# Quantised feed-forward stage: second norm's moments at the GELU on ScalarE, the output norm's last pass on ScalarE, the next batch's first norm ahead of the second norm

## The reference

```
def act_quant_fake(x):
    scale = 127.0 / jnp.clip(jnp.max(jnp.abs(x), axis=-1, keepdims=True), 1e-05)
    return jnp.clip(jnp.round(x * scale), -128.0, 127.0) / scale
...
h = layernorm(x, ln1_g, ln1_b)      # 256 features: "first norm"
h = bitlinear(h, w1, b1)            # act_quant_fake(h) @ ternary w1 + b1, 256 -> 1024
h = jax.nn.gelu(h, approximate=False)
h = layernorm(h, ln2_g, ln2_b)      # 1024 features: "second norm"
h = bitlinear(h, w2, b2)            # 1024 -> 256
...
x = _layernorm(x + _L1_ffn_ref(x, ...), axis=-1)   # "output norm", no gain or offset
```

## Time and profile before

| | |
|---|---|
| median of the runs | 3598.76 us (three runs: 3587.14, 3598.76, 16188.73) |
| the profiled execution | 3601.07 us |
| its span, first to last instruction | 3599.3 us |
| instructions | 49730 |
| TensorE busy | 2938.0 us (82%) |
| VectorE busy | 2760.9 us (77%) |
| ScalarE busy | 1921.6 us (53%) |
| GpSimd busy | 2071.5 us (58%) |

### The profile page before, as it was taken

The page is one execution under the profiler, slowest core; times in us unless marked ns, Lnnn a source line. Parts: engine busy times, 40 slices in busy tenths (PEclk is TensorE's granted clock), DMA queues, the critical chain, the costliest instruction groups (busy, mean ns, idle before and its releaser), DMA issues. The chain is left out here.

```text
span 3599.3 us, 49730 instructions
## 1 busy us (share of the span) xinstructions
PE 2938.0 (82%) x18386; PEld 1618.9 (45%) x18386; DVE 2760.9 (77%) x4668; ACT 1921.6 (53%) x3233; POOL 2071.5 (58%) x1116
## 2 busy tenths in 40 slices
PE   8968989657489748899999999999999999758633
PEld 3438888534367513344444443444434444234412
DVE  4566767666411129999999999999999999967588
ACT  2343333214211127678777777778777787524244
POOL 0015445312400116989999999999999999932100
PEclk8878888769699869999999999999999999978856
DMA  1000000000323243444444454444544444420000
GB/s 51 0 1 3 4 4 4 8 21 0 120 93 128 68 117 118 156 145 173 155 146 154 148 175 155 145 158 146 176 155 148 152 153 149 149 95 1 22 0 24
DMA packets 120572, 343.63 MB, mean 95 GB/s; under 512 B 14875, under 2 KB 45554, under 8 KB 119570
## 3 DMA queue, kind: packets, MB, share of 16 engines
q1 hardware_dynamic: 114450, 331.91, 27.5%
q0 software_dynamic: 3072, 6.00, 0.8%
q10 hardware_dynamic: 2816, 2.62, 0.2%
HBM read 328.21 MB, written 14.68 MB: 95 GB/s over the span
## 5 line engine op out<-in xcount | busy, mean ns | idle before, releaser
L2034 POOL TENSOR_TENSOR mb_h<-mb_h,mb_BC 128x1024 f32<-128x1024 f32 x512 | 1218.0, 2399 | 195.8 <-DVE mb_h L2326 194.6
L2326 DVE TENSOR_TENSOR_SCAN mb_h<-mb_dA,mb_bx 128x512 f32<-128x512 f32 x1024 | 1183.1, 1192 | 47.1 <-ACT mb_dA L2189 47.1
L2422 PE MATMUL mb_y<-mb_h,ident 128*128 128x512 f32 x2048 | 943.0, 605 | 57.0 <-POOL mb_h L2034 56.7
L2189 ACT ACTIVATE mb_dA<-mb_delta,mb_A 128x511 f32<-128x511 f32 x1024 | 658.0, 713 | 175.0 <-DVE mb_h L2326 171.6
L2322 DVE TENSOR_TENSOR mb_bx<-mb_du,mb_BC 128x512 f32<-128x512 f32 x1024 | 646.7, 673 | 1.9 <-ACT mb_du L2133 1.9
L2422 PEld LDWEIGHTS mb_y<-mb_h,ident 128*128 128x128 f32 x2048 | 380.5, 192 | 581.4 <-issue 422.9
L250 PE MATMUL mb_p<-mb_xT,mb_in_w 128*128 128x512 f32 x512 | 269.6, 676 | 87.7 <-ACT mb_sz L2093 81.1
L250 PE MATMUL mb_p<-mb_upad,mb_convd 128*128 128x512 f32 x512 | 225.0, 592 | 0.8 <-ACT mb_upad L2081 0.8
L250 PEld LDWEIGHTS mb_p<-mb_xT,mb_in_w 128*128 128x128 f32 x512 | 110.1, 219 | 239.7 <-issue 136.7
L1738 DVE TENSOR_TENSOR me_h<-me_s,me_p 128x320 f32<-128x320 f32 x64 | 31.2, 488 | 220.8 <-ACT me_s L1715 220.8
L1692 POOL DMA_INDIRECT me_y<-expert_results,slot x32 | 31.1, 973 | 258.1 <-DMA expert_results<-me_oe 248.7
(11 more groups left out here) (443 smaller groups left out, 5534.7 us busy)
## 6 DMA issues: line engine op xcount, KB each, us to landing
mb_BC<-mamba_BC SPq DMA_DIRECT2D x256, 1024.0 KB, 5.3
me_W<-in_L_ffn_W SPq DMA_DIRECT2D x24, 1024.0 KB, 9.4
mb_in_w<-in_L_attn_in_proj_w SPq DMA_DIRECT2D x4, 1024.0 KB, 5.1
mb_convd<-in_mamba_taps SPq DMA_DIRECT2D x4, 1024.0 KB, 7.2
expert_rows<-me_zero SPq DMA_DIRECT2D x1, 2560.0 KB, 10.1
x<-in_x SPq DMA_DIRECT2D x4, 512.0 KB, 5.5
me_xe<-expert_rows SPq DMA_DIRECT2D x8, 256.0 KB, 10.6
expert_results<-me_oe ACTq DMA_DIRECT2D x8, 256.0 KB, 7.6
```

The source lines that it names most:

```text
L2034: tt(hk, hk, buffer(k, it)[:, 1, :, :], ALU.mult).then_inc(*pos(f"hc_{k}{part}"))
L2189: i = av(dA[k % 2][:, c, s, 1:], delta[:, it % 2, mc, 1:], ACT.Exp, scale=A[:, MC * layer(it) + mc, n:n + 1])
L2326: nc.vector.tensor_tensor_scan(h[k % NBUF][:, c, s, :], dA[k % 2][:, c, s, :], bx[s][:, :], 0.0, ALU.mult, ALU.add).then_inc(*dvs(f"sc{s}_ ...
L2422: i = mm(ybank[c][:, :], m.ident[:, :], h[k % NBUF][:, c, s, :], start=False, stop=e == HALF - 1 and s == SU - 1)
```

## The change

- The second norm's moments are taken on ScalarE. Each GELU also sums its output into `sums`; a Copy makes minus the mean of it (`mv[:, q, 0:1]`), and a Square of h2 with that as bias sums the squared deviations into `mv[:, q, 1:2]`. `second_stats` and its semaphore are gone. `second_sqrt` takes the root with scale 1/1024 and epsilon as bias. `affine` adds the (negative) mean of the second norm where it subtracted it.
- `last_norm` is split: VectorE makes the reciprocal and `shift`, minus mean times reciprocal; ScalarE makes the four passes of 128x256 as x * rstd + shift.
- On VectorE `first_quantised(b+1)` stands ahead of `second_norm(b)`.
- On ScalarE `second_sqrt(b+1)` stands directly behind `gelu(b+1)`, and `last_norm(b-1)` ahead of `scaled(b)`.

```diff
@@ -2831,7 +2831,8 @@
-        stats, mv, sd, rstd = (sb(f"qf_{n}", s) for n, s in (("stats", [P, TPB, 2, 6]), ("mv", [P, TPB, 2]), ("sd", [P, TPB]), ("rstd", [P, TPB])))
+        sums, mv, sd, rstd = (sb(f"qf_{n}", s) for n, s in (("sums", [P, TPB]), ("mv", [P, TPB, 2]), ("sd", [P, TPB]), ("rstd", [P, TPB])))
+        squares, eps, shift = sb("qf_squares", [P, HF]), sb("qf_eps", [P, 1]), sb("qf_shift", [P, TPB])
...
@@ -2867,7 +2868,7 @@
-                    sp.wait_ge(*dve3.at("out", b))
+                    sp.wait_ge(*act4.at("out", b))
@@ -2891,11 +2892,18 @@
                 def gelu(j):
                     for q in tl:
                         a.wait_ge(*dve_e.at(f"e{q}", j))
-                        av(h2[:, j % 2, q, :], h2[:, j % 2, q, :], ACT.Gelu).then_inc(*act1(f"g{q}"))
+                        if q == 0:
+                            a.wait_ge(*dve2.at(f"g{TPB - 1}", j - 1))
+                        av(h2[:, j % 2, q, :], h2[:, j % 2, q, :], ACT.Gelu, accum_out=sums[:, q:q + 1]).then_inc(*act1(f"g{q}"))
+                        a.wait_ge(*act1.at(f"g{q}", j))
+                        av(mv[:, q, 0:1], sums[:, q:q + 1], ACT.Copy, scale=-1.0 / HF).then_inc(*act1(f"m{q}"))
+                        a.wait_ge(*act1.at(f"m{q}", j))
+                        av(squares[:, :], h2[:, j % 2, q, :], ACT.Square, bias=mv[:, q, 0:1], accum_out=mv[:, q, 1:2]).then_inc(*act1(f"v{q}"))
 
                 def second_sqrt(b):
-                    a.wait_ge(*dve_st.at("eps", b))
-                    av(sd[:, :], sd[:, :], ACT.Sqrt).then_inc(*act2("sqrt"))
+                    a.wait_ge(*act1.at(f"v{TPB - 1}", b))
+                    a.wait_ge(*dve2.at("rstd", b - 1))
+                    av(sd[:, :], mv[:, :, 1], ACT.Sqrt, scale=1.0 / HF, bias=eps[:, 0:1]).then_inc(*act2("sqrt"))
 
                 def scaled(b):
                     a.wait_ge(*dve2.at("rec", b))
@@ -2918,8 +2926,15 @@
                     a.wait_ge(*dve3.at("eps", b))
                     av(lnc.sd[:, :], lnc.sd[:, :], ACT.Sqrt).then_inc(*act4("sqrt"))
 
+                def last_norm(b):
+                    a.wait_ge(*dve3.at("shift", b))
+                    for q in tl:
+                        i = av(tile(b, q), tile(b, q), ACT.Identity, scale=lnc.rstd[:, q:q + 1], bias=shift[:, q:q + 1])
+                    i.then_inc(*act4("out"))
+
                 first_sqrt(0)
                 first_half(0)
+                a.wait_ge(ident_made, 1)
                 gelu(0)
                 second_sqrt(0)
                 for b in range(B):
@@ -2931,16 +2946,21 @@
                         last_sqrt(b - 1)
                     if more:
                         gelu(b + 1)
+                        second_sqrt(b + 1)
+                    if b and more:
+                        last_norm(b - 1)
+                    if more:
                         scaled(b)
-                        second_sqrt(b + 1)
                     cast(b)
                     if more:
                         copies(b)
+                last_norm(B - 2)
                 last_sqrt(B - 1)
+                last_norm(B - 1)
 
             @block.vector
             def _(v):
-                begin(v, dve_s, dve1, dve_e, dve_st, dve2, dve3)
+                begin(v, dve_s, dve1, dve_e, dve2, dve3)
                 tt, stt, tsc = nc.vector.tensor_tensor, nc.vector.scalar_tensor_tensor, nc.vector.tensor_scalar
 
                 def first_stats(j):
@@ -2955,10 +2975,10 @@
                     v.wait_ge(*dve_s.at("mean", j))
                     tsc(lna.sd[:, :], lna.mv[:, :, 1], LN_EPS, None, ALU.add).then_inc(*dve_s("eps"))
 
-                def affine(dve, j, src, h, mean, inverse, gain, offset):
+                def affine(dve, j, src, h, mean, centre, inverse, gain, offset):
                     v.wait_ge(*dve.at("rstd", j))
                     for q in tl:
-                        stt(h(q), src(q), mean[:, q, 0:1], gain, ALU.subtract, ALU.mult).then_inc(*dve(f"g{q}"))
+                        stt(h(q), src(q), mean[:, q, 0:1], gain, centre, ALU.mult).then_inc(*dve(f"g{q}"))
                     for q in tl:
                         v.wait_ge(*dve.at(f"g{q}", j))
                         stt(h(q), h(q), inverse[:, q:q + 1], offset, ALU.mult, ALU.add).then_inc(*dve(f"n{q}"))
...
@@ -2993,25 +3013,11 @@
                             i = stt(h2[:, j % 2, q, cols], bank[2 * (q % 2) + half][:, :], q1["inv"][:, q:q + 1], rows["b1"][:, cols], ALU.mult, ALU.add)
                         i.then_inc(*dve_e(f"e{q}"))
 
-                def second_stats(b):
-                    v.wait_ge(*dve2.at(f"g{TPB - 1}", b - 1))
-                    for q in tl:
-                        v.wait_ge(*act1.at(f"g{q}", b))
-                        for half in range(2):
-                            i = nc.vector.bn_stats(stats[:, q, half, :], h2[:, b % 2, q, half * 512:half * 512 + 512])
-                    i.then_inc(*dve_st("stats"))
-                    v.wait_ge(*dve_st.at("stats", b))
-                    for q in tl:
-                        i = nc.vector.bn_aggr(mv[:, q, :], stats[:, q, :, :])
-                    i.then_inc(*dve_st("mean"))
-                    v.wait_ge(*dve_st.at("mean", b))
-                    tsc(sd[:, :], mv[:, :, 1], LN_EPS, None, ALU.add).then_inc(*dve_st("eps"))
-
                 def second_norm(b):
                     v.wait_ge(*act2.at("sqrt", b))
                     nc.vector.reciprocal(rstd[:, :], sd[:, :]).then_inc(*dve2("rstd"))
                     h = lambda q: h2[:, b % 2, q, :]
-                    affine(dve2, b, h, h, mv, rstd, rows["g2"][:, :], rows["b2n"][:, :])
+                    affine(dve2, b, h, h, mv, ALU.add, rstd, rows["g2"][:, :], rows["b2n"][:, :])
 
                 def second_largest(b):
                     v.wait_ge(*actr.at(f"r{TPB - 1}", b - 1))
@@ -3041,7 +3047,7 @@
-                    v.wait_ge(*dve3.at("out", b - 1))
+                    v.wait_ge(*act4.at("out", b - 1))
@@ -3056,10 +3062,9 @@
                     v.wait_ge(*act4.at("sqrt", b))
                     nc.vector.reciprocal(lnc.rstd[:, :], lnc.sd[:, :]).then_inc(*dve3("rstd"))
                     v.wait_ge(*dve3.at("rstd", b))
-                    for q in tl:
-                        i = tsc(tile(b, q), tile(b, q), lnc.mv[:, q, 0:1], lnc.rstd[:, q:q + 1], ALU.subtract, ALU.mult)
-                    i.then_inc(*dve3("out"))
-
+                    stt(shift[:, :], lnc.mv[:, :, 0], -1.0, lnc.rstd[:, :], ALU.mult, ALU.mult).then_inc(*dve3("shift"))
+
+                nc.vector.memset(eps[:, :], LN_EPS)
                 nc.vector.tensor_copy(identb[:, :], m.ident[:, :]).then_inc(ident_made, 1)
                 first_stats(0)
                 v.wait_ge(norm_in, 32)
@@ -3068,12 +3073,10 @@
                 first_products(0)
                 for b in range(B):
                     more = b + 1 < B
-                    second_stats(b)
                     if more:
                         first_stats(b + 1)
+                        first_quantised(b + 1)
                     second_norm(b)
-                    if more:
-                        first_quantised(b + 1)
                     second_largest(b)
                     if not more:
                         last_scaled()
```

More of the change, by code:

```diff
@@ L2843, in quantised_ffn @@
         pe1, pe2 = signal("tensor_1", "h1T " + each("h")), signal("tensor_2", "h2T0 " + " ".join(f"h2T{q + 1} o{q}" for q in tl[:-1]) + f" o{TPB - 1}")
-        act0, act1, act2 = signal("scalar_0", "sqrt"), signal("scalar_1", "q h1T " + each("g")), signal("scalar_2", "sqrt")
-        actr, act3, act4 = signal("scaled", each("r")), signal("scalar_3", each("q")), signal("scalar_4", "sqrt")
+        act0, act1, act2 = signal("scalar_0", "sqrt"), signal("scalar_1", "q h1T " + each("g", "m", "v")), signal("scalar_2", "sqrt")
+        actr, act3, act4 = signal("scaled", each("r")), signal("scalar_3", each("q")), signal("scalar_4", "sqrt out")
         acth = signal("copies", each("h2T"))
@@ L2848, in quantised_ffn @@
         dve1 = signal("vector_1", "rstd " + groups("g", "n") + " max clip rec " + each("low") + " inv")
-        dve_e, dve_st = signal("vector_e", each("e")), signal("vector_stats2", "stats mean eps")
+        dve_e = signal("vector_e", each("e"))
         dve2 = signal("vector_2", "rstd " + groups("g", "n") + " max clip rec inv")
-        dve3 = signal("vector_3", "res b2 stats mean eps rstd out")
+        dve3 = signal("vector_3", "res b2 stats mean eps rstd shift")
         row = lambda n, w: rows[n][:, :].rearrange("p (o n) -> p o n", o=1).broadcast_to([P, TPB, w])
@@ L2977, in first_quantised @@
                     v.wait_ge(*act1.at("q", j - 1))
-                    affine(dve1, j, lambda q: tile(j, q), lambda q: h1[:, q, :], lna.mv, lna.rstd, rows["g1"][:, :], rows["b1n"][:, :])
+                    affine(dve1, j, lambda q: tile(j, q), lambda q: h1[:, q, :], lna.mv, ALU.subtract, lna.rstd, rows["g1"][:, :], rows["b1n"][:, :])
                     largest(dve1, j, full(h1), q1)
```

## The result

The changed kernel takes 3629.19 us (median of 4 runs, 3624.74 to 3631.20), the kernel before 3594.17 us in the same comparison. The ratio is 1.0099, with a 95% interval of 1.0080 to 1.0118: 0.99% slower, some 35 us. It lies within the 2% that count as no change here, but its interval is well clear of 1. 3633 was predicted, 3617 to 3648 the range.

What follows compares the result with a forecast made beforehand. VectorE was taken to bound the last stage, busy 165.0 of 189 us. Delays of + 33.2 us up to second_products(2) and + 0.9 in the tail made + 34.1 on the median of 3598.76: 3633 us, range 3617 to 3648.

Steps and rivals of the forecast that it cites:

- The place of the wait: VectorE, ahead of first_quantised: waits for ScalarE's first norm root, 21.2 us in batch 1 and 23.2 in batch 2.
- A tile of 2.6 us: ScalarE: GELU, accumulator read, Copy and Square of one tile take 2.6 us, bounds 2.1 to 3.0.
- Batches: Last stage, from one first_products to the next: 55.6 and 57.6 us, against 41.24 for a middle batch before.
- The wait for TensorE ahead of second_products(2): VectorE in batch 3: a wait of about 1.4 us for TensorE's last product.
- The tail: From second_products(2) to the end: 0.9 us longer, from a later and slower last pass of the output norm.
- a sign of being wrong that the prediction named: ScalarE's cast and copies, without VectorE's work beside them, taking another time than 11.4 us; 1 us off allowed.
- the 34.1 of the sum: Last stage: total added time, + 33.2 us up to second_products(2) and + 0.9 in the tail.
- The drain of the page: ScalarE table loads: the skill page adds about 1.38 us of drain at each, about 5.5 us for four.
- rival 2: ScalarE's table drain is paid four times ahead of VectorE's second_norm: 3638 us, chance 0.05.
- No gain, no loss: Batch 0: second_stats is replaced by a wait of its length; next first_products at 3461.5, before 3461.16.
- The rival on the other side: First norm's root not late: change wins if VectorE's wait is below 6.8 us; 3588 us, chance 0.06.

Runs made afterwards that it cites:

- e1: The change with the first norm's root of batch b+2 on ScalarE directly behind the second norm's root of batch b+1: 3594.05 us, ratio 1.0000.
- e3: The kernel before with only VectorE's order changed, first_quantised(b+1) ahead of second_norm(b): 3613.54 us, ratio 1.0057.
- e9: The change with ScalarE's wait for the identity moved from ahead of the first GELU to ahead of the first root: 3628.23 us (one run).
- e6: The change with first_stats and its root one batch earlier, scaled(b) ahead of batch b+1's GELUs, and the identity's wait ahead of everything: 3580.30 us, ratio 0.9956.
- e2: The change with VectorE's order put back, second_norm(b) ahead of first_quantised(b+1): 3616.69 us, ratio 1.0051.
- e4: The change without the second norm's moments on ScalarE, mean and variance being constants: 3606.42 us, ratio 1.0037.
- e8: The change with the output norm's last pass back on VectorE: 3628.16 us, ratio 1.0091.

## Why the prediction was right

- *The place of the wait and its mechanism.* VectorE waits for the first norm's root in batches 1 and 2, released by ScalarE: 21.2 and 23.2 us predicted, 21.26 and 22.72 measured. e1 shows that this root's place on ScalarE is what the wait hangs on, and e3 that VectorE's order makes more than half of the loss without any work moved.
- *The amounts on ScalarE.* A tile of 2.6 us: 2.54 to 2.57. From the first GELU to the end of the second root 12.0: 11.9 (3514.07 to 3525.98). last_norm 2.0: 1.97 (3525.88 to 3527.85). The rows of another stage, with the passes of 1024 columns beside them, gave this to 0.1 us. That Square and Copy bring no table load of their own was read from the instruction order and is so: there are eight loads in the stage.
- *Batches.* 55.6 and 57.6 us predicted, 55.99 and 57.61 measured. The wait for TensorE ahead of second_products(2) was to be 1.4 and is 1.57:

```profile
3602.94 1.66 DVE L3045 SCALAR_TENSOR_TENSOR x<-qf_o,qf_inv,x 128x256 f32<-128x256 f32 x4 [1.57 <-PE qf_o L250]
```

- *The tail* was to be + 0.9, and is + 0.5 (3602.94 to 3628.7 is 25.76, before 25.29). The 0.9 are there from second_products(3) on (11.1 us, from 3617.62, against 10.2); the way to it is 0.4 shorter.
- *Parts that cancelled.* That batch 1's wait came out within 0.1 us is luck in part. The first GELU starts 1.4 us behind first_products in batches 1 and 2 and not 1.6, and moments and root take 11.8 up to the next instruction and not 12.0; but cast and copies take 11.7 to the first norm's reciprocal (3474.42 to 3486.11, 3532.37 to 3544.07) and not 11.4. That was a sign of being wrong that the prediction named; it is 0.3 us, within the 1 us allowed for. The fourth tile's transposes took 1.06 us in all three batches of the change, and 0.84, 0.70 and 0.61 before.
- *The total* is 3.8 us off, and that says little. The stage grew by 35.3 us, 1.2 more than the 34.1 of the sum. The profiled span is nevertheless 3628.7 and not 3633.4, because the five stages ahead were 5.95 us shorter in this execution (3420.59 against 3426.54), and the 3633 stood on a median of 3598.76, where the comparison has 3594.17.
- *The drain of the page* (the Trainium skill, ScalarE: Activation LUTs, "What ACT_TABLE_LOAD costs"). It would have had about 1.4 us more at each load. The load starts at 3524.38, 0.01 us behind the accumulator's read, and last_norm, behind the root, at 3525.88: 1.50 us for load and root, of which the load is 1.28. No drain shows here either, and rival 2 falls.
- *Batch 0, the term that was mis-sized.* "No gain, no loss" between the first two first_products: predicted + 0.3 us, measured + 1.4. I had the first GELU 1.4 us behind first_products, as before; it is 2.8 (3420.59 to 3423.35), because the table load there had taken on the wait. e9 shows it. With these 1.3 us the sum of 34.1 is 35.4, and the stage grew by 35.3. That they meet so closely is luck again: batch 1 has 0.4 more than worked out and batch 3 up to second_products(2) 0.2 more, and the tail 0.4 less.

```profile
3420.59 2.95 DVE L3013 SCALAR_TENSOR_TENSOR qf_h<-qf_p,qf_inv,qf_b 128x512 f32<-128x512 f32 x4 [5.48 <-PE qf_p L250]
```

- *The rival on the other side* had its deciding point right and its condition wrong. A middle batch wins when the wait is under 6.8 us: in e1 it is 5, and its batches are 0.4 and 1.6 us shorter than before; in e6 it is 0, and with the rest of the order the kernel is 0.44% faster. But the prediction held it enough for 3588 that ScalarE does the root ahead of cast and copies. e1 does just that and came out level at 1.0000: there the root still stands behind the moments, which are 10 us long. In e6, which gains, first_stats and the root stand ahead of the moments; no run has these alone.

## What to carry to other kernels

On engines that run in order, ask for every instruction that another engine waits for what stands ahead of it in its queue, above all for the small ones: here a root of 0.2 us stood behind 29.8 us of other work (3514.07 to 3543.84), and its consumer, with 7.3 us of its own to do in that time, waited 22.7. When a step is moved ahead on its engine, move its inputs ahead on the others in the same edit, and ask what it used to cover. An offload should be judged only after the order fits it: the same moved work was + 0.99% in one order and - 0.44% in another.

## What was unexpected of the hardware

**A table load can take on a wait.** With the identity's wait ahead of the first GELU, the load ran behind the first tile of first_products and not ahead of it (the rows of the change and of e9 above), and the GELU started 1.3 us later than in e9. In batch 1 the load took on another wait, for the second norm of the batch before:

```profile
3446.98 1.28 ACT L2897 ACT_TABLE_LOAD   x1 [1.87 <-DVE qf_h L2981]
```

It cost nothing, since the GELU behind it waited 9.82 us more for first_products; in batches 2 and 3 no wait of the load shows. Read side by side, the timelines of all eleven kernels have one pattern: the GELU itself waits for what stands first among its waits in the program, and the load ahead of it for what stands next. Where the identity stands first, the load waits for first_products (the change, e1, e2, e4 and e8, 3.62 or 3.63 us each); where first_products stand first or alone, it does not. This is read from the releasers, and no run was made to try it.

**TensorE's granted clock differed in the same work.** The fourth tile's eight transposes between cast and copies stand in the timeline of the change as

```profile
3475.61 2.07 PE L3120 MATMUL qf_t<-qf_identb,qf_h2q 128*128 128x128 bf16 x16 [14.13 <-ACT qf_h2q L2917]
...
3483.87 1.06 PE L3120 MATMUL qf_t<-qf_identb,qf_h2q 128*128 128x128 bf16 x8
```

and in that of e9 as

```profile
3475.11 2.07 PE L3120 MATMUL qf_t<-qf_identb,qf_h2q 128*128 128x128 bf16 x16 [13.91 <-ACT qf_h2q L2917]
...
3482.92 0.61 PE L3120 MATMUL qf_t<-qf_identb,qf_h2q 128*128 128x128 bf16 x8
```

1.06 against 0.61 us, and the granted clock of the stretch was 0.54 in the change (3474.4 to 3485.9) and 0.59 in e9 (3473.4 to 3484.5), as a share of full speed. Both are near the lower level, 1.2 GHz, with more of e9's stretch at 2.4. TensorE had waited 14.13 and 13.91 us before the two. In batch 2 it had waited 15.87 us in both kernels, and the fourth tile's transposes took 1.06 and 0.63. So the idle time ahead does not tell them apart, and I have no run that says what does. From the start of cast to the start of the first root are 11.46 us in the change and 10.57 in e9: that is the 0.9 us of e9's batch 1 which its edit does not explain. In batch 2 they are 11.47 and 11.04, which is its 0.4; of the 0.5 behind batch 2, 0.1 is found in the third such stretch (transposes of 1.06 against 0.95) and 0.3 in the last batch, where eight of TensorE's products took 1.55 against 1.23.
